# Turning an expert's gathered rows by one transposing DMA, and keeping the row weights later

## What is computed

```python
buf = zeros((e, cap, d)).at[e_flat, posc].add(where(keep, xf[tok], 0))      # gather
h   = gelu(einsum('ecd,edf->ecf', buf, w1) + b1)
out = einsum('ecf,efd->ecd', h, w2) + b2
y   = zeros((n, d)).at[tok].add(w * out[e_flat, posc])                      # scatter-add
```

## Time and profile before

| what | before |
|---|---|
| median of 3 runs | 2440.32 us |
| lowest and highest run | 2434.68 and 2441.76 us |
| span of the profiled execution | 2439.8 us |
| its own time | not listed apart from the three runs |
| start of the expert stage's first load | 1546.5 us |
| busy: VectorE, ScalarE | 1597.8 us (65%), 1146.7 us (47%) |
| mean granted clock of TensorE | 0.981 |

### The profile page before, as it was taken

How to read it: one execution, slowest core, us unless ns; L and a number is a source line. 1 busy time by engine, 2 the same in 40 slices (tenths; PEclk the granted TensorE clock), 3 DMA queues, 4 the chain that set the end, 5 groups by cost and what they waited for, 6 DMA issues and landing times. The chain is left out here.

```text
span 2439.8 us, 48490 instructions
## 1 busy us (share of the span) xinstructions
PE 2294.5 (94%) x17681; PEld 1669.9 (68%) x17681; DVE 1597.8 (65%) x3339; ACT 1146.7 (47%) x1634; POOL 146.4 (6%) x144
## 2 busy tenths in 40 slices
PE   1899999999999999999889998599999999999998
PEld 1788888888888888888735544356565656556563
DVE  5767877788787778777856677446454545545450
ACT  2654554455555545554533334346453535445450
POOL 0000000000000000000002222101101010101101
PEclk9999999999999999999999999699999999999999
DMA  8000000000000000000355543323233342423221
GB/s 316 19 10 36 35 9 34 34 34 34 26 34 15 28 34 34 34 17 27 123 193 220 213 172 110 119 78 103 82 123 118 116 116 73 112 77 108 83 82 22
DMA packets 71934, 198.51 MB, mean 81 GB/s; under 512 B 8272, under 2 KB 8400, under 8 KB 63684
## 3 DMA queue, kind: packets, MB, share of 16 engines
q1 hardware_dynamic: 60996, 177.22, 19.7%
q0 software_dynamic: 10880, 20.52, 4.3%
HBM read 133.08 MB, written 71.52 MB: 84 GB/s over the span
## 5 line engine op out<-in xcount | busy, mean ns | idle before, releaser
L1066 PE MATMUL ps<-arena 128*128 (+1 forms) x4992 | 574.7, 273 | 7.3 <-DVE arena L653 7.3
L1055 PE MATMUL ps<-arena 128*128 128x256 f16 x4992 | 576.7, 274 | 1.5 <-DVE arena L608 1.5
L1066 PEld LDWEIGHTS ps<-arena 128*128 128x128 f16 x4992 | 487.6, 98 | 73.8 <-issue 14.1
L1055 PEld LDWEIGHTS ps<-arena 128*128 128x128 f16 x4992 | 490.1, 98 | 64.0 <-DVE arena L608 2.8
L1717 PE MATMUL ps<-arena 128*128 128x320 f16 x3072 | 426.1, 302 | 15.9 <-ACT arena L1667 14.7
L1734 PE MATMUL ps<-arena 128*128 128x512 f16 x1920 | 420.3, 379 | 0.0
L1717 PEld LDWEIGHTS ps<-arena 128*128 128x128 f16 x3072 | 302.1, 99 | 139.8 <-ACT arena L1667 17.0
L1734 PEld LDWEIGHTS ps<-arena 128*128 128x128 f16 x1920 | 186.2, 98 | 218.3
L918 ACT ACTIVATE arena<-ps,arena (+1 forms) x192 | 148.9, 776 | 331.2 <-PE ps L1055 329.7
L1451 PE MATMUL ps<-arena 128*128 128x512 f16 x1080 | 243.5, 384 | 3.6 <-PEq L436 3.2
L624 DVE TENSOR_TENSOR arena<-arena 128x512 f32<-128x512 f32 x192 | 132.4, 689 | 144.4 <-ACT arena L918 108.8
(11 more groups left out here) (220 smaller groups left out, 1796.2 us busy)
## 6 DMA issues: line engine op xcount, KB each, us to landing
arena<-in_L_ffn_w SPq DMA_DIRECT2D x64, 1024.0 KB, 9.7
arena<-feats SPq DMA_DIRECT2D x16, 1536.0 KB, 6.6
arena<-in_x SPq DMA_DIRECT2D x32, 512.0 KB, 5.7
feats<-arena SPq DMA_DIRECT2D x16, 1024.0 KB, 3.9
rows<-arena SPq DMA_DIRECT2D x1, 10320.0 KB, 30.0
arena<-rows SPq DMA_DIRECT2D x8, 1290.0 KB, 5.8
feats<-arena SPq DMA_DIRECT2D x16, 512.0 KB, 2.6
out<-arena SPq DMA_DIRECT2D x16, 512.0 KB, 2.8
```

The lines of the kernel that those rows point to most:

```text
L1055: mm = pe.matmul(out, ctxT[:, s, k, (2 * t + h) * P:(2 * t + h + 1) * P], qT[:, r, k, :], start=(k == 0 and s + r == 0), stop=(k == KD - 1 ...
L1066: mm = pe.matmul(psA[:, k, :], ctxN[:, 2 * t + h, s, k * P:(k + 1) * P], prob[:, bass.ds(a % 3, 1), r, h, :].rearrange("p o i -> p (o i)") ...
```

## The change

- `Xr`, its load and its bitcast, `turn`, `turned`, the PSUM banks `psX` and the semaphores of the turns are gone.
- SyncE fills `XT` straight from DRAM by one transposing DMA per expert (`turn_rows`): source 640 rows of 1024 f16 values, which lie 2064 bytes apart; destination 128 partitions x 8 x 640. For expert 0 it is the first DMA of the stage, for e + 1 it is issued when layer 1 of e is done, behind w1's and ahead of w2's loads.
- The 4 words of information get a tile `info` of their own and a small DMA (`load_info`), issued at the top of the loop, once `weights_of(e)` has read the tile.
- TensorE's `layer_1` waits for the transposing DMA (`xt_loaded`) in place of the ScalarE copies.
- `keep_weights(e)`, with its wait for the scatter-adds of e - 1, moves from the end of `layer_2` of e - 1 to f = 14 of `layer_1` of e (not for expert 0). VectorE's loop is turned by half a step for that. TensorE's loop takes all eight experts.

```diff
-    XT = take([2, KD, CAP], F16)
-    Xr = take([ST, ROW], F32)
-    Xh = Xr.bitcast(F16)
+    XT = take([2, KD, CAP], F16, off[0] + -off[0] % 16)
+    off[0] += -off[0] % 16 + KD * CAP
+    info = take([ST, 4], F32)
...
-            def load_rows(e):
-                sp.dma_start(Xr, rows[bass.ds(e * CAP, CAP), :].rearrange("(t p) c -> p t c", p=P))\
-                    .then_inc(x_loaded, 16)
+            def load_info(e):
+                sp.dma_start(info, rows[bass.ds(e * CAP, CAP), D:D + 4].rearrange("(t p) c -> p t c", p=P))\
+                    .then_inc(info_loaded, 16)
+
+            def turn_rows(e):
+                sp.dma_start_transpose(XT.rearrange("p s k c -> p (s k) c"),
+                                       rows[bass.ds(e * CAP, CAP), 0:D].bitcast(F16)).then_inc(xt_loaded, 16)
...
-            load_rows(0)
+            turn_rows(0)
+            load_info(0)
             load_b2(0)
             sp.wait_ge(s_lo, CH)
             ew.load(sp, 0, True)
             with sp.Fori(0, E - 1) as e:
-                sp.wait_ge(a_step, AK * (e + 1))
+                sp.wait_ge(a_step, AK * e + 5)
                 apart(sp, sp_passed)
-                sp.wait_ge(x_turned, ST * (e + 1))
-                load_rows(e + 1)
+                load_info(e + 1)
                 sp.wait_ge(s_lo, CH * (2 * e + 2))
                 ew.load(sp, e + 1, False)
+                sp.wait_ge(h_done, KF * (e + 1))
+                turn_rows(e + 1)
                 sp.wait_ge(s_lo, CH * (2 * e + 3))
                 ew.load(sp, e + 1, True)
...
-            def layer_1(e):
+            def layer_1(e, first=False):
                 for f in range(KF):
                     n = e * KF + f
+                    if f == 14 and not first:
+                        dve.wait_ge(added, 16 * ST * e)
+                        keep_weights(e)
...
             weights_of(0)
             keep_weights(0)
+            layer_1(0, first=True)
             with dve.Fori(0, E - 1) as e:
-                layer_1(e)
                 layer_2(e)
                 weights_of(e + 1)
-                dve.wait_ge(added, 16 * ST * (e + 1))
-                keep_weights(e + 1)
-            layer_1(E - 1)
+                layer_1(e + 1)
             layer_2(E - 1, more=False)
...
             def layer_2(e, more=True):
                 for t in range(ST):
                     n = e * ST + t
-                    if more:
-                        turned(e + 1, t)
...
             def layer_1(e):
-                pe.wait_ge(xt_ready, ST * (e + 1))
+                pe.wait_ge(xt_loaded, 16 * (e + 1))
                 pe.wait_ge(s_lo, CH * (2 * e + 1))
...
-                    if more:
-                        turn(e + 1, t)
```

More of the change, by code:

```diff
@@ L1509, in experts @@
     NT = out.shape[0]
-    take, _ = cutter(arena[:, :EARLY])
+    take, off = cutter(arena[:, :EARLY])
     hT = take([KF, 2, CAP], F16)
-    XT = take([2, KD, CAP], F16)
-    Xr = take([ST, ROW], F32)
-    Xh = Xr.bitcast(F16)
+    XT = take([2, KD, CAP], F16, off[0] + -off[0] % 16)
+    off[0] += -off[0] % 16 + KD * CAP
+    info = take([ST, 4], F32)
     h32 = [take([CAP], F32) for _ in range(2)]
@@ L1523, in experts @@
     al, tk = [take([ST], F32) for _ in range(2)], [take([ST], U32) for _ in range(2)]
-    ident = cst["ident"]
     b1T, en, inv1, inv2, sh, s_step, s_lo = ew.b1T, ew.en, ew.inv1, ew.inv2, ew.sh, ew.s_step, ew.s_lo
@@ L1528, in experts @@
     psO = ps[:, 4:6, :]
-    psX = [ps[:, n, :].bitcast(F16).rearrange("p (c i) -> p c i", i=P) for n in (6, 7)]
     with ExitStack() as st:
@@ L1533, in sem @@
             return st.enter_context(nc.semaphore(name))
-        x_loaded, x_turned, xt_ready, a_step = (sem(s) for s in ("rows_loaded", "x_turned", "xt3_ready", "a_step"))
+        info_loaded, xt_loaded, a_step = (sem(s) for s in ("info_loaded", "xt_loaded", "a_step"))
         h_done, g_done, h_hi, h_lo = (sem(s) for s in ("h_done", "g_done", "h_hi", "h_lo"))
@@ L1593, in weights_of @@
                 s = Steps(dve, a_step, e, AK)
-                info = Xr[:, :, D:D + 4]
-                dve.wait_ge(x_loaded, 16 * e + 16)
+                dve.wait_ge(info_loaded, 16 * e + 16)
                 s.step(dve.tensor_copy(tk[0], info[:, :, 0:1].bitcast(U32).rearrange("p t o -> p (t o)")))
@@ L1653, in _ @@
         def _(act):
[L1654 to L1657, removed]
             def layer_1(e):
@@ L1676, in layer_2 @@
                     n = e * ST + t
-                    if more:
-                        turned(e + 1, t)
-                        if t in (2, 3):
-                            for c in range(4):
-                                ew.high_part(act, 2 * e + 2, 4 * (t - 2) + c, False)
+                    if more and t in (2, 3):
+                        for c in range(4):
+                            ew.high_part(act, 2 * e + 2, 4 * (t - 2) + c, False)
                     act.wait_ge(o_bias, n + 1)
@@ L1685, in layer_2 @@
                     act.mul(oa[t % 2], o32[t % 2], al[1][:, t:t + 1]).then_inc(o_scaled, 1)
-            for t in range(ST):
-                turned(0, t)
             with act.Fori(0, E - 1) as e:
@@ L1720, in layer_1, with layer_2 @@
                     mm.then_inc(h_done, 1)
-            def layer_2(e, more=True):
+            def layer_2(e):
                 pe.wait_ge(s_lo, CH * (2 * e + 2))
@@ L1737, in layer_2 @@
                     mm.then_inc(o_done, 1)
-            for t in range(ST):
-                turn(0, t)
-            with pe.Fori(0, E - 1) as e:
+            with pe.Fori(0, E) as e:
                 layer_1(e)
                 layer_2(e)
-            layer_1(E - 1)
-            layer_2(E - 1, more=False)
 def gated_layer(nc, x, ctx, g_x, g_f, w_sim, b_sim, w_qv, b_qv, w_r, b_r, w1, b1, w2, b2, out):
```

## The result

The changed kernel takes 2400.26 us (median of 4 runs, 2399.02 to 2402.18) against 2439.88 us before: a ratio of 0.9846, interval 0.983 to 0.9861. The forecast was 2406 us, range 2396 to 2430. The profiled execution took 2399.04 us with a span of 2397.3.

The account below looks back on a forecast made before the run. TensorE, busy 94% of the span, was taken as the bound. Span 2439.8 - 15.7 - 14.7 - 4.8 + 0.5 - 0.4 + 1.1 = 2405.8, so time 2406 us, range 2396 to 2430.

Parts of the forecast that it names:

- The turns leave the path: Expert stage: 35 blocks of transposes at 0.45 us each leave TensorE's path, 15.7 us.
- The late copy frees the head: Heads of layer 1: TensorE's 14.7 us of waits for the Gelu and 4.8 us at low clock go.
- What should be late next: Layer 1's head after the late copy: w2's maximum, then h's low halves; first Gelu ready with 0.7 us of slack.
- T = 12 us for the transposing DMA: Issue to landing: 2.4 us fixed plus 9.6 us for 320 runs per engine at 30 ns; bounds 5.9 to 42.7 us.
- Hidden behind layer 2: Experts 1 to 7: the transposing DMA has 45.5 us of layer 2 left after w1's loads, so it costs nothing.
- Cold start: Expert 0's layer 1 starts at clock 0.50: 2.5 us lost (1.6 to 4.8) against 1.4 before, so +1.1.
- a unit price: Layer 1 of one expert, 384 matmuls on TensorE, undisturbed: 52.39 us.
- the half microsecond that the sum calls rounding: Expert stage: the itemised losses made 36.6 us against the 36.1 us target; the excess entered the span as +0.5.
- The low end of the range: Whole kernel: DMA time 5.9 us and 1.6 us lost cold give 2399, runs up to 5.6 us under their median: 2396.
- Rival A: Before layer 1: the transposing DMA outlasts layer 2, past 46 us; slower, 2505 us at 160 ns per run; chance 0.13.
- B: Expert 0's start: transposing DMA takes 25 to 46 us, paid once; 2429 us at 35 us; chance 0.10.
- C: Layer 1's head: the stall stays through w2's first chunk or the table load; 14.7 + 4.8 us stay, 2425 us; chance 0.06.

Follow-up runs that it names:

- Experiment 1: The kernel before with only the late copy of the row weights, TensorE still turning the rows: 2420.55 us, ratio 0.9925.
- experiment 7: The changed kernel with expert 0's transposing DMA cut into two of 320 rows, layer 1 beginning on the first half, another chip: 2417.83 us, ratio 0.9834.
- experiment 3: The changed kernel with the transposing DMA of experts 1 to 7 done four times in a row: 2400.13 us, ratio 0.9841.
- experiment 2: The changed kernel with the row weights copied at the end of layer 2 again, so only the transposing DMA is new: 2416.02 us, ratio 0.9901.
- Experiment 4: The changed kernel with the transposing DMA of experts 1 to 7 done eight times in a row: 2574.71 us, ratio 1.0553.
- experiment 5: The changed kernel with eight transposing DMAs in a row and the scatter-adds of all experts left out: 2478.86 us, ratio 1.0164.
- experiment 9: The changed kernel unaltered, five runs on one chip beside its best version: 2399.82 us, ratio 0.9841 to the kernel before.
- Experiment 6: The changed kernel with 24 unused matmuls on TensorE during the first transposing DMA, on another chip: 2418.47 us, ratio 0.9834.

## Why the prediction was right

*The turns leave the path* (15.7 us): right. Experiment 1 still has them, and its stretch is 15.4 us longer than the changed kernel's.

*The late copy frees the head* (14.7 + 4.8 us): right, shown by experiment 1 alone, where the waits and the three clock falls are gone. What should be late next wasn't: the low halves of h run directly behind ScalarE, as worked out. One reading on the way was too early: the working let w2's first load land 4.9 us after its issue, the quickest landing of its rows. It lands some 7.3 us after it (1653.68 to 1661.0), and VectorE waits 1.1 us for it. The first low half still waits 1.69 us for ScalarE, so nothing was lost. The working treated the two parts as independent; together they are worth 36.07 us, one after the other 20.7 and 15.4 or 20.1 and 16.0, so what each is worth depends on the order by 4.7 us, and the sum of the whole doesn't.

*T = 12 us for the transposing DMA*: the step that failed, as a size. Expert 0's took 7.41 us. The count behind it was right: SyncE's queue has 102212 packets against 60996, 41216 more for 8 experts, 5152 each (the 640 small ones of `info` stand in for the 640 of the plain load), where I had counted 5120 runs of 256 bytes. The price per run was not: at 290 GB/s one engine moves 18.1 GB/s, a run costs 14 ns, not the 30 that I drew from a stretch in which packets of 4 bytes passed between large ones; why a packet was dearer there no run shows. 320 x 14 is 4.5 us, and 2.9 are left. That these are a fixed part agrees with experiment 7, where half the rows take 5.06 us, 2.25 and 2.8. So layer 1 of expert 0 began 7.56 us after the issue, and the start gained 4.9 us, not 0.4. Of the two pages of the Trainium skill that the prediction sets against each other, "as fast as regular ones" is nearer, but the rate is a quarter lower here. 1309 ns per block, one after another, falls: 40 blocks took 7.41 us, 0.19 each. A third place of the Trainium skill fits better ("DMA: Bandwidth & Descriptors", Latency and other measured facts): it gives such DMAs 261 GB/s, some 30% lost, where the middle dimension isn't contiguous, and about 350 to 400 GB/s in the contiguous case. The trace shows 290 against 392, 26% under; which of the two cases this transfer is, no run here tells.

*Hidden behind layer 2*: right, with room. The median from issue to landing is 11.5 us, w1's loads ahead included, and experiment 3 hides four of them.

*Cold start* (2.5 us lost): 1.97 (54.13 - 52.16), within the bounds that I gave. It differs between profiles of the same start: the first layer 1 takes up to 54.98 us in experiments 2 to 5 and 9, a loss of 2.8. Experiment 6 shows that it is the clock, since TensorE kept busy by unused matmuls gives it back.

Of the 8.5 us between the forecast span (2405.8) and the span, 4.6 are T, 1.5 the earlier stages, 0.5 the cold start, and 1.8 a unit price: I took 52.39 us for an undisturbed layer 1 from a piece behind a wait, and it is 52.16. That price also hid 1.3 us which the seven waits cost beside their own length (13.05 + 39.29 us around a wait), so the half microsecond that the sum calls rounding was not rounding. The low end of the range doesn't follow from its own terms: 2399 us less 5.6 is 2393, not 2396; the measured 2400.26 us lies inside both.

*Rival A* didn't come true, but its price would have been too low. It let a longer DMA grow by its own time alone, although the working names the scatter-adds beside it. Experiment 4 shows that DMAs which last through layer 2 meet the five scatter-adds, and paid 23 us per expert in place of 12. *B* fell by T, *C* by experiment 1.

## What to carry to other kernels

A turn that TensorE does on its critical path can be given to a DMA where a stage of several times its length lies between issue and use; price it by the packets that it makes and, if it is long, by what else is on the DMA engines then. Look for waits that protect a buffer nobody reads yet: copying it later in the same queue was worth half the gain (20.7 of 41 us beside the turns, 16.0 without them). Where a stage starts cold, the wait for its first DMA is time in which unused matmuls cost nothing, as long as they end before it lands: 16 of them ended 1.3 us too late.

## What the runs showed of the hardware that was not expected

A transposing DMA of 1.3 MB moves 290 GB/s alone and takes 6.8 to 7.6 us from issue to landing; with a scatter-add beside it, up to 11.5 us, and the scatter-adds beside four turns per expert land in 8.0 us (median) in place of 5.0. It holds the SyncE queue for 5.0 to 5.3 us alone, and 9.4 to 9.7 us behind w1's loads in the changed kernel. A wait of TensorE of about 2 us costs the clock at some times and not at others: the seven waits of before (0.96 to 2.63 us) gave three falls, the seven of experiment 2 (0.94 to 2.18 us) gave one.
